# Handovers of a fused four-stage kernel: who stores the last expert tiles, what the first gather signals, and where eight groups of 16-wide inverses are made

## The reference, cut to what matters

```python
x = x + sum over the 2 chosen experts of gate * expert(x)
h = layernorm(x)
q, k, v = silu(short_conv(h @ Wq)), ...             # taps over 4 tokens
attn = where(strict_lower, -(k_beta @ k.T), 0)      # 32 x 32 of each chunk and head
for i in range(1, 32):
    attn[i, :i] = attn[i, :i] + attn[i] @ attn[:, :i]
attn = attn + eye(32)                               # (1 - L)^-1
u = attn @ v; w = attn @ k_beta
for each chunk in order:                            # S: 64 x 64 of each head
    u_adj = u - w @ S
    o = q @ S + where(lower_incl, q @ k.T, 0) @ u_adj
    S = S + k.T @ u_adj
x = x + rms_norm(o) @ Wo
```

## Time and profile before

| | |
|---|---|
| runs before, us | 1562.38 median of 3 (1562.16 to 1563.25) |
| profiled execution | 1563.12 us, its span 1561.4 us |
| busy | PE 83%, DVE 58%, POOL 38%, ACT 31% of the span |
| first layer | until about 609 us |
| delta_inputs | 618.6 to 1060 us |
| delta_rule | 1060 to about 1380 us |

### The profile page before, as it was taken

The page is one execution under the profiler, slowest core; times in us unless marked ns, Lnnn a source line. Parts: engine busy times, 40 slices in busy tenths (PEclk is TensorE's granted clock), DMA queues, the critical chain, the costliest instruction groups (busy, mean ns, idle before and its releaser), DMA issues. The chain is left out here.

```text
span 1561.4 us, 35775 instructions
## 1 busy us (share of the span) xinstructions
PE 1298.7 (83%) x11893; PEld 946.6 (61%) x11894; DVE 909.2 (58%) x2019; ACT 487.5 (31%) x1181; POOL 600.1 (38%) x787
## 2 busy tenths in 40 slices
PE   7999999899999994566576678306999999979997
PEld 6888888567777773233243344205888888845555
DVE  6788888342222221588887787872566666634443
ACT  1112121322222221255565556301222222213332
POOL 3435666135111111687778657501233333310000
PEclk9999999899999998698898888655899999969999
DMA  9999500123111112113233222145232232300001
GB/s 314 348 354 342 189 32 33 47 88 122 61 60 60 60 60 66 57 63 92 84 97 99 81 70 85 60 72 130 76 103 93 87 107 89 102 1 18 28 28 36
DMA packets 177075, 156.08 MB, mean 100 GB/s; under 512 B 65640, under 2 KB 154216, under 8 KB 176968
## 3 DMA queue, kind: packets, MB, share of 16 engines
q1 hardware_dynamic: 154360, 127.83, 26.0%
q0 software_dynamic: 9552, 26.10, 5.0%
q10 hardware_dynamic: 13056, 0.79, 0.5%
HBM read 64.22 MB, written 90.44 MB: 99 GB/s over the span
## 5 line engine op out<-in xcount | busy, mean ns | idle before, releaser
L928 PE MATMUL ps_sc<-w,a_qeo 128*128 x568 | 183.4, 466 | 0.0
L736 DVE TENSOR_TENSOR a_stm<-a_vpad,ps_sc 128x352 f32<-128x352 f32 x71 | 37.0, 521 | 177.4 <-ACT a_vpad L500 159.8
L409 POOL DMA_DIRECT2D x_slots<-a_stm x71 | 39.0, 549 | 243.1 <-issue 241.0
L928 PEld LDWEIGHTS ps_sc<-w,a_qeo 128*128 128x128 f32 x568 | 104.1, 193 | 46.5 <-issue 2.5
L1629 PE MATMUL d_pp<-d_xT,d_w_p 128*128 128x512 f32 x192 | 105.3, 685 | 26.3 <-ACT d_xT L1321 25.3
L1491 DVE SCALAR_TENSOR_TENSOR d_cout<-d_cin,d_taps,d_cout 128x512 f32<-128x512 f32 x144 | 124.6, 868 | 3.8
L898 PE MATMUL ps_kv<-w,a_stm 128*128 x426 | 105.8, 384 | 1.1 <-DVE a_stm L729 1.1
L2347 PE MATMUL g_pp<-g_xT,g_w_g 128*128 128x512 f32 x192 | 90.8, 613 | 8.4 <-ACT g_xT L2238 8.4
L898 PEld LDWEIGHTS ps_kv<-w,a_stm 128*128 128x128 f32 x426 | 79.4, 190 | 30.2 <-issue 12.7
L1629 PEld LDWEIGHTS d_pp<-d_xT,d_w_p 128*128 128x128 f32 x192 | 39.6, 221 | 67.1 <-issue 36.6
L2084 PE MATMUL u_bank_g<-u_qkT 64*128 64x128 f32 x512 | 40.8, 304 | 44.7 <-DMA u_kve<-rec 44.7
(11 more groups left out here) (277 smaller groups left out, 3009.0 us busy)
## 6 DMA issues: line engine op xcount, KB each, us to landing
x_slots<-a_zeros SPq DMA_DIRECT2D x32, 1024.0 KB, 10.8
u_kve<-rec SPq DMA_DIRECT2D x32, 384.0 KB, 3.3
a_qeo<-x_slots SPq DMA_DIRECT2D x71, 128.0 KB
x_slots<-a_stm POOLq DMA_DIRECT2D x71, 128.0 KB
rec<-d_ve SPq DMA_DIRECT2D x32, 256.0 KB, 2.1
rec<-d_bT SPq DMA_DIRECT2D x32, 256.0 KB, 2.2
u_qkT<-rec SPq DMA_DIRECT2D x32, 256.0 KB, 2.8
w<-in_w SPq DMA_DIRECT2D x4, 1408.0 KB, 14.8
```

The costliest lines, as they stand in the source:

```text
L928: mm = pe.matmul(ps, e_xT[:, q, k, :], w13[:, s, k, bass.ds(e_hidden, 1), :], start=(k == 0), stop=(k == KD - 1))
```

## The change

1. **Last expert stores.** The last 5 of the 71 stores (from tile `HAND` = 66) are issued by SP with semaphores of their own, `ey_last`. The weight loads of the second stage and the wait for `t_cleared` stand ahead of SP's expert loads.
2. **First gather.** The gathers of group 0 signal a semaphore per tile, `got_first[j]`; DVE waits for each tile's own two transfers.
3. **Straight steps.** `singly` makes all steps of delta_inputs straight on all engines, and the first 16 tiles of delta_rule (8 before).
4. **Inverses.** `PART` is [0, 3, 8]. Groups 0 to 2 are inverted in the last step of delta_inputs, in the places where groups 0 to 5 were. Groups 3 to 7 are inverted by DVE in steps 0 to 7 of the delta rule (`ROWS_AT`), between stm and share, and sent by SP behind the loads of tiles 9, 10 and 11 (`SEND_AT`); the wait for these sends stands ahead of tile 12. `l_in` and `l_back` live across both stages, and the rule has a `prod` of its own.
5. **Sends.** `send_inverses` makes 4 transfers a group of 64x16x16 instead of 16 of 16x16x16. For this `t_mat` is laid out by group and head, and the load of `x0` takes 4 pieces of 64 values for each token.

```diff
-def pipelined(eng, n, depth, step, ahead=0, unroll=2):
-    lo = -(-(depth + 1) // unroll) * unroll
+def pipelined(eng, n, depth, step, ahead=0, unroll=2, singly=0):
+    lo = -(-max(depth + 1, singly) // unroll) * unroll
     hi = n - ahead - (n - ahead - lo) % unroll
+    if hi <= lo:
+        for i in range(n + depth):
+            step(i, i % unroll)
+        return
...
+        HAND = N - (N - KNOWN) % 2 - EDEPTH
...
+                t, q = j - 4, par
+                if isinstance(j, int) and HAND <= t < N:
+                    sp.wait_ge(ey_out, t + 1)
+                    sp.dma_start(x_slots[row_of(sp, t), :], e_y[:, q, :]).then_inc(ey_last[q], 16)
+
+            kept_loads = load_delta_weights(sp, kept, w, kept_loaded)
+            sp.wait_ge(t_cleared, 16)
...
-            kept_loads = load_delta_weights(sp, kept, w, kept_loaded)
+            for q in range(2):
+                sp.wait_ge(ey_last[q], 16 * len(range(HAND + q, N, 2)))
             sp.wait_ge(kept_loaded, kept_loads)
-            sp.wait_ge(t_cleared, 16)
...
-PART = [0, 6, NG]
+PART = [0, 3, NG]
+ROWS_AT = {0: (1, 6), 1: (6, 9), 2: (9, 11), 3: (11, 12), 4: (12, 13), 5: (13, 14), 6: (14, 15), 7: (15, 16)}
+SEND_AT = {9: (3, 4), 10: (5, 6), 11: (7,)}
...
-SENDS = 16
+SENDS = 4
...
-    for h in range(NH1):
-        for z in range(2):
-            r = 64 * s + 16 * h
-            dst = t_mat[u * GW:(u + 1) * GW, :].rearrange("(b s i) (h z w c) -> s w h z b i c", s=2, i=SUB, h=NH1, z=2, w=2)
-            eng.dma_start(dst[s, s, h, z], t_out[r:r + 16, u, :, z, :]).then_inc(sent, 16)
+    for z in range(2):
+        dst = t_mat[u].rearrange("h (b s i) (z w c) -> s w z (h b) i c", s=2, i=SUB, z=2, w=2)
+        eng.dma_start(dst[s, s, z], t_out[64 * s:64 * s + 64, u, :, z, :]).then_inc(sent, 16)
...
+                            .then_inc(got_first[j] if isinstance(u, int) and u == 0 else got_in[q], 16)
...
-                if j == 0:
-                    wait(dve, got_in[par], 16 * 8 * ((i - par) // 2 + 1) if isinstance(i, int) else 64 * (i - par) + 128)
+                if isinstance(i, int) and i == 0:
+                    dve.wait_ge(got_first[j], 32)
...
-            pipelined(dve, NG, DEPTH, step)
+            pipelined(dve, NG, DEPTH, step, singly=NG)
...
+                if isinstance(i, int) and i in ROWS_AT:
+                    lo, hi = ROWS_AT[i]
+                    if lo == 1:
+                        dve.wait_ge(l_back[1], 16 * 8 * (NG - PART[1]))
+                    inverse_rows(dve, t_out, l_in, prod, sub_own, 1, lo, hi)
+                    if hi == SUB:
+                        dve.wait_ge(sub_own, 30)
+                        dve.tensor_copy(t_out[:, PART[1]:NG, :, 1, :],
+                                        t_out[:, PART[1]:NG, :, 0, :].rearrange("p g i c -> p g c i")).then_inc(sub_done, 1)
```

More of the change, by code:

```diff
@@ L485, in estep @@
                     act.wait_ge(ey_done, t + 1)
-                    wait(act, ey_sent[q], 8 * (t - q))
+                    if isinstance(t, int) and t - 2 >= HAND:
+                        act.wait_ge(ey_last[q], 16 * len(range(HAND + (q - HAND) % 2, t, 2)))
+                    else:
+                        wait(act, ey_sent[q], 8 * (t - q))
                     act.activation(e_y[:, q, :], ps_y, ACT.Copy).then_inc(ey_out, 1)
@@ L1051, in inverses_in, with inverse_rows, delta_inputs @@
                              .rearrange("p g (i z c) -> p g i z c", i=SUB, z=2)
-SENDS = 16
+SENDS = 4
 def send_inverses(eng, t_out, t_mat, u, s, sent):
-    for h in range(NH1):
-        for z in range(2):
-            r = 64 * s + 16 * h
-            dst = t_mat[u * GW:(u + 1) * GW, :].rearrange("(b s i) (h z w c) -> s w h z b i c", s=2, i=SUB, h=NH1, z=2, w=2)
-            eng.dma_start(dst[s, s, h, z], t_out[r:r + 16, u, :, z, :]).then_inc(sent, 16)
-def delta_inputs(nc, kept, loaded, got, t_sent, x_res, gates, slots, x_slots, small, rec, l_mat, t_mat):
+    for z in range(2):
+        dst = t_mat[u].rearrange("h (b s i) (z w c) -> s w z (h b) i c", s=2, i=SUB, z=2, w=2)
+        eng.dma_start(dst[s, s, z], t_out[64 * s:64 * s + 64, u, :, z, :]).then_inc(sent, 16)
+def inverse_rows(dve, t_out, l_in, prod, sub_own, n, lo, hi):
+    groups = slice(PART[n], PART[n + 1])
+    count = PART[n + 1] - PART[n]
+    inv = t_out[:, groups, :, 0, :]
+    for row in range(lo, hi):
+        if row > 1:
+            dve.wait_ge(sub_own, 2 * (row - 1))
+        a = prod[:, 0:count, 0:row, 0:row]
+        dve.tensor_tensor(a, l_in[:, groups, row:row + 1, 0:row].broadcast_to([P, count, row, row]),
+                          inv[:, :, 0:row, 0:row].rearrange("p g j k -> p g k j"), ALU.mult).then_inc(sub_own, 1)
+        dve.wait_ge(sub_own, 2 * row - 1)
+        dve.tensor_reduce(inv[:, :, row, 0:row], a, AX.X, ALU.add).then_inc(sub_own, 1)
+def delta_inputs(nc, kept, loaded, got, l_in, l_back, t_sent, x_res, gates, slots, x_slots, small, rec, l_mat, t_mat):
     with ExitStack() as ctx:
@@ L1199, in step @@
                         wait_apart(sp, loaded, l_sent[j], 16 * (u + 1))
-                    back = l_back[1 if isinstance(u, int) and u >= PART[1] else 0]
+                    back = l_back[0 if isinstance(u, int) and u < PART[1] else 1]
                     for s in range(2):
@@ L1207, in step @@
                                          src[s, h, s]).then_inc(back, 16)
-            pipelined(sp, NG, DEPTH, step, ahead=1)
+            pipelined(sp, NG, DEPTH, step, singly=NG)
             sp.wait_ge(sub_done, 1)
@@ L1302, in step @@
                     mix_conv(u, q)
-            pipelined(pool, NG, DEPTH, step, ahead=1)
+            pipelined(pool, NG, DEPTH, step, singly=NG)
         @block.scalar
@@ L1423, in step @@
                     silu(u, q, 1)
-            pipelined(act, NG, DEPTH, step)
+            pipelined(act, NG, DEPTH, step, singly=NG)
             act.wait_ge(sub_done, 1)
@@ L1436, in _, with rows @@
             dve.wait_ge(zeroed, 4)
-            def rows(n, lo, hi):
-                groups = slice(PART[n], PART[n + 1])
-                count = PART[n + 1] - PART[n]
-                inv = t_out[:, groups, :, 0, :]
+            def rows(lo, hi):
                 if lo == 1:
@@ L1529, in step @@
                 if last:
-                    rows(0, 1, 6)
+                    rows(1, 6)
                 if here:
@@ L1536, in step @@
                 if last:
-                    rows(0, 6, 9)
+                    rows(6, 9)
                 if here:
@@ L1543, in step @@
                 if last:
-                    rows(0, 9, 11)
+                    rows(9, 11)
                 if tiles:
@@ L1555, in step @@
                 if last:
-                    rows(0, 11, 13)
+                    rows(11, 13)
                 if here:
@@ L1593, in step @@
                 if last:
-                    rows(0, 13, SUB)
-                if isinstance(i, int) and i == NG + 2:
-                    rows(1, 1, SUB)
-            pipelined(dve, NG, DEPTH, step)
+                    rows(13, SUB)
+            pipelined(dve, NG, DEPTH, step, singly=NG)
         @block.tensor
@@ L1832, in step @@
                     sp.dma_start(kve[:, k], row[:, 0:3 * D].rearrange("p (n c) -> p n c", n=3)).then_inc(rec_in[k], 16)
-            pipelined(sp, NT, DEPTH, step, unroll=4)
+                if isinstance(t, int) and t in SEND_AT:
+                    if t == min(SEND_AT):
+                        sp.wait_ge(sub_done, 1)
+                    for u in SEND_AT[t]:
+                        for s in range(2):
+                            send_inverses(sp, t_out, t_mat, u, s, t_sent[1])
+            pipelined(sp, NT, DEPTH, step, unroll=4, singly=GROUP * PART[1] + 1)
             gate_loads = load_gate_weights(sp, gate_kept, w, gates_loaded)
@@ L1925, in step @@
                     z.then_inc(s_out, 1)
-            pipelined(act, NT, DEPTH, step, unroll=4)
+            pipelined(act, NT, DEPTH, step, unroll=4, singly=GROUP * PART[1] + 1)
         @block.vector
@@ L2402, in build @@
         t_sent = [ctx.enter_context(nc.semaphore(f"t_sent{n}")) for n in range(2)]
[L2403 removed]
+        l_in = ctx.enter_context(nc.sbuf_tensor("l_in", [P, NG, SUB, SUB], F32))
+        l_back = [ctx.enter_context(nc.semaphore(f"l_back{n}")) for n in range(2)]
+        delta_inputs(nc, kept, kept_loaded, got, l_in, l_back, t_sent, x_res, gates, slots, x_slots, small, rec, l_mat, t_mat)
         gate_kept = gate_weights(nc, ctx)
[L2405 removed]
+        delta_rule(nc, kept, gate_kept, kept_loaded, got, l_in, l_back, t_sent, x_res, small, rec, l_mat, t_mat, w)
         gated_output(nc, gate_kept, kept["ident"], kept_loaded, x_res, out)
```

58 lines of the change are left out of this document (28 added, 30 removed).

## The result

| | before | after |
|---|---|---|
| runs, us | 1562.5 median of 4 (1562.2 to 1563.3) | 1537.1 median of 4 (1536.9 to 1537.9) |
| profiled execution, us | 1563.1 | 1537.0 |
| span, us | 1561.4 | 1535.3 |

The ratio is 0.984 (0.982 to 0.986): 25 us or 1.6% faster. The forecast was 1525, 37 us faster, with a range of 1513 to 1537; the measured time lies 0.1 us beyond its upper end.

A forecast was written before the change was run, and what follows sets the result against it. PE, busy 83% of the span, was taken as the bound over long stretches, with stage handovers as its longest waits. Terms -8.5 - 0.9 - 10.5 - 9.6 - 16.8 + 9 = -37.3 from 1563.1 gave about 1525 us, range 1513 to 1537.

The forecast's parts named there:

- the first handover: Between expert stores and next stage: POOL's drain moves beside PE's last tiles, -8.5 us (0 to -9.5).
- the wait for `zeroed`: At DVE's first add: POOL's memsets behind all eight gathers limit the gain from per-tile signals to -0.9 us.
- the straight steps: In delta_inputs: straight steps take 43.73 us, loop steps 46.5; -10.5 us, ends -4 and -12.
- the inverses in delta_inputs: DVE's last step there: three groups instead of six and a shorter copy, -9.6 us, ends -7 and -11.
- the rule's start: Steps 1 and 2 of the delta rule: 6.3 us of rows against 4.5 us of DVE waiting, +2.5 with the start-up.
- the lower end, 4 us: In delta_inputs: only the idle times at loop turns are regained, -4 for -10.5; as a rival 10%, 1532.
- the sends: Copy's end to the rule's first load: 12 transfers with half the pieces, 8.8 us instead of 25.6, -16.8.
- at the work done per piece they need 6.7 us with the engines full: Sends: 8.75 ns of an engine per piece, from the 0.56 busy share, gives 6.7 us for 12,288 pieces.
- the rows in the rule: Steps 5 to 7 of the delta rule: DVE's rows stick out by 1.5, 1.9 and 3.4 us, +6.8.
- so what sticks out is paid in full: Delta rule: PE waits for DVE's work behind the rows, so sticking-out rows cost their length, +6.8 in steps 5 to 7.
- a rival in which it rises later: Delta rule: DVE's rows keep PE's clock low three more steps, 13.7 us less the 6.8; 1532, chance 12%.
- The two small terms that cancel in the forecast: At the rule: x0's 512 pieces instead of 128 cost 0.3 us at first load; fewer loop turns give -0.3; together 0.

The follow-up runs named there:

- e4_pool: The changed kernel with the last five expert stores on POOL again, weight loads still ahead of SP's expert loads; 1545.0 us.
- e7_zero: The changed kernel with POOL's four memsets between the first tile's gathers and the rest; 1533.7 us.
- e5_loops: The changed kernel with the hardware loop of delta_inputs back on POOL, ACT, DVE and PE, SP staying straight; 1548.4 us.
- e6_part6: The changed kernel with groups 0 to 5 inverted in delta_inputs, only 6 and 7 in the rule, and sends of the new form; 1539.6 us.
- e3_oldsends: The changed kernel with 16 sends a group of 16x16x16 as before, in place of 4 of 64x16x16; 1557.0 us.
- e1_norows: The changed kernel without the inverses of groups 3 to 7 in the rule, only row 1 and a one-value-a-row copy left; 1519.3 us.
- e2_early: The changed kernel with the same rows of inverses, but all in steps 0 to 4 of the delta rule; 1536.0 us.
- f1_poolcols: The changed kernel with the inverses of groups 3 to 7 on POOL instead of DVE, by columns, in steps 0 to 8 of the rule; 1520.1 us.
- g1_dvecols: The changed kernel with the inverses of groups 3 to 7 on DVE in the same place, but by columns; 1531.4 us.
- h2_pause: The changed kernel with the copy behind the first lot of inverses made four times, a 4.5 us pause ahead of the rule; 1539.6 us.
- f2_all: The changed kernel with groups 3 to 7 inverted on POOL by columns, the first lot on DVE by columns, and memsets behind the first tile's gathers; 1499.8 us.
- h1_nozero: The fastest version (columns on POOL in the rule, columns on DVE in delta_inputs, early memsets) without the early memsets; 1503.6 us.
- h3_bestpause: The fastest version (columns on POOL and DVE, early memsets) with a 4.5 us pause ahead of the rule, the copy made four times; 1516.3 us.

## Why the prediction was wrong

**Right, within 1 us each:** the first handover (-8.1 for -8.5, and the uncovered drain of e4_pool), the wait for `zeroed` that takes what the tiles' signals could bring (e7_zero), the straight steps (-10.2 for -10.5, e5_loops), the inverses in delta_inputs (-9.0 for -9.6; the rows of three groups take 14.9 us, the number forecast, but the copy took 1.44 us again and not 0.8) and the rule's start (+2.3 for +2.5). The rule of the Trainium skill on sequential fetch (Runtime: NRT & Kernel Launch, section "Instruction fetch mechanics") gave the lower end, 4 us; the four intervals shrank by 10.7 from before and grew by 9.4 in e5_loops, so most of it isn't in the turns.

**Wrong in size, -14.1 for -16.8: the sends.** The mechanism held; the step that failed is "at the work done per piece they need 6.7 us with the engines full". Full engines take 1,320 small pieces a us, not 1,830, as e6_part6 shows, which makes 9.3 us; a share of 0.56 didn't mean that 0.44 was room. By the rule of the Trainium skill that issue on several engines saves only the sequencer's time, small beside the transfer (DMA: Bandwidth & Descriptors, section "Issuing engines are not separate DMA queues"), the phase would have been 14.1 us. With the old form it was 13.8, but 11.9 of them went to the issues themselves (e3_oldsends), so small they aren't there; with the new form it was 11.6.

**Wrong in the sum, +11.4 for +6.8: the rows in the rule.** The sizes held: steps 5 to 7, for which "1.5, 1.9 and 3.4" were forecast, stuck out by 1.7, 1.3 and 4.0, in all 7.1 for 6.8 (that the total is so near is in part luck, the single steps miss by up to 0.6). The step that failed is "so what sticks out is paid in full": it was paid in full and more. PE stands still 3.7 us behind row 15 and the copy, its clock falls, and the next two steps at the low clock cost 2.7 and 2.1 more, a term that the sum didn't have. I had the clock only as a rival in which it rises later, while here it rose 42 us behind the first product, where before it was 39, and fell again. That the fall needs the rows and the copy in DVE's stream at the high clock is shown by e1_norows, e2_early and f1_poolcols, in none of which it falls there; in all eight traces with five groups of inverses on DVE up to step 7 it falls within 3 us of that step's share, which comes anywhere from 1089 to 1111.

**Not in the sum at all, +4.1: the last two steps.** Their work is untouched, and the sum had no term for them. The step that failed is that it took them as unchanged; the clock falls 12 us sooner in them. They are slow in every changed kernel with rows of inverses on DVE in the rule (e2_early, e6_part6, g1_dvecols, h2_pause among them), and there the clock falls 6.4 to 7.6 us behind the third last share. They are fast in before, e1_norows, f1_poolcols, f2_all and h1_nozero, with the fall 19.1 to 19.9 us behind that share; h3_bestpause lies between (15.2 us, intervals 8.52 and 8.29), with no rows on DVE in the rule. Why rows over 200 us earlier should matter is open; that only the point of time decides is argued, not shown. The 1.7 us gained behind the last share are unexplained too; the low clock there ends 26.8 us behind that share before and 24.7 after. The two small terms that cancel in the forecast, -0.3 and +0.3, show in no run by themselves.

The balance of the edit: making the second lot in the rule's DVE stream cost 18 us (e1_norows, 1519.3, with the low clock that follows). All the rest of the change earned 43.

## What to carry to other kernels

Work moved into a stage that PE bounds should go to an engine that waits long in one place (POOL here, 19.5 us of work for under 1 us), in pieces shorter than the waits that it is put ahead of; the price of one burst too long isn't only its length (4.0 us here) but also the low clock behind it (4.7). A stop of PE at the high clock, 3.7 us here, has to be priced with a fall of the clock. And before many small transfers are put on a queue, count the queue's time per transfer (0.57 us here) against the loads that stand behind them, not only the bytes.
